# Padding the selector and the transposed weights of a windowed attention from 48 to 128 rows

## The reference, cut to what matters

```python
ak = (ax @ WK_w + WK_b).reshape(Bx, 1, nh, d)
av = (ax @ WV_w + WV_b).reshape(Bx, 1, nh, d)
pad_k = jnp.pad(k, ((0, 0), (1, 1), (0, 0), (0, 0)))
k_shift = jnp.stack([pad_k[:, t:Lx + t] for t in range(3)], axis=3)
K = jnp.concatenate([akb, k_shift], axis=3)
V = jnp.concatenate([avb, k_shift], axis=3)
scores = jnp.einsum('blhd,blhjd->blhj', q, K) / jnp.sqrt(jnp.float32(d))
alphas = jax.nn.softmax(scores, axis=-1)
att = jnp.einsum('blhj,blhjd->blhd', alphas, V).reshape(Bx, Lx, nh * d)
return att @ WO_w + WO_b
```

## Time and profile before

| | us |
|---|---|
| median of 3 runs | 2455.49 (2452.77 to 2458.71) |
| the profiled execution, device time | 2449.27 |
| its span, first to last instruction | 2447.5 |
| the attention stage that the change touches | about 740 to 1127 of the span |

### The profile page before, as it was taken

One profiled execution on the slowest core, in us unless ns is written; L12 is line 12 of the kernel. 1 busy time (PEld: TensorE's weight loads), 2 busy tenths in 40 slices (PEclk: granted clock), 3 DMA queues, 4 the chain that ended last, 5 costly groups with the idle time before them and its releaser, 6 DMA issues.

```text
span 2447.5 us, 74401 instructions
## 1 busy us (share of the span) xinstructions
PE 2164.3 (88%) x31577; PEld 1391.1 (57%) x31577; DVE 1746.2 (71%) x4002; ACT 1072.9 (44%) x2881; POOL 455.4 (19%) x791
## 2 busy tenths in 40 slices
PE   7999898899778889887899999967888789999988
PEld 5555544444454545453566666755665567777665
DVE  3443598999656777776777877826888667777776
ACT  2333255666531112112555555543444455555544
POOL 2211000000003242332011111244231111111100
PEclk9899799999787888876999999958999689999999
DMA  2000000000100000002111111016452211111111
GB/s 57 4 3 4 1 1 1 1 2 1 36 16 2 3 2 3 2 2 78 52 37 37 41 41 38 26 27 125 92 98 50 61 37 49 39 40 40 40 48 31
DMA packets 76109, 77.47 MB, mean 32 GB/s; under 512 B 15768, under 2 KB 57072, under 8 KB 74192
## 3 DMA queue, kind: packets, MB, share of 16 engines
q1 hardware_dynamic: 71872, 70.21, 11.3%
q10 hardware_dynamic: 3904, 2.49, 0.3%
HBM read 60.19 MB, written 11.82 MB: 29 GB/s over the span
## 4 chain that ended last, share of the span: by engine, by line
PE 32%; DVE 14%; ACT 6%; issue 4%; DMA 1%; SPq 0%; POOL 0%; ACTq 0%; DVEq 0%; POOLq 0%
PE B L85 31%; DVE work L2031 4%; DVE work L107 2%; ACT hr L103 2%; DVE work L2035 1%; DVE hr L2022 1%; ACT L103 1%; ACT ltc L103 1%; ACT work L103 1%; ACT catt L103 1%; DVE lpq L107 1%; DVE lth L107 1%; ACT lth L103 1%; DVE catt L2326 0%; DVE lh L107 0%
## 5 line engine op out<-in xcount | busy, mean ns | idle before, releaser
L85 PE MATMUL B<-gr,wres 128*128 128x512 f32 x1248 | 380.0, 428 | 30.9 <-DVE work L107 12.7
L85 PEld LDWEIGHTS B<-gr,wres 128*128 128x128 f32 x1248 | 230.3, 194 | 113.8 <-DVE work L107 39.3
L2076 POOL COPY G<-lh 128x32 f32<-128x32 f32 x256 | 148.0, 578 | 770.5 <-DVE lh L107 770.5
L103 ACT ACTIVATE work<-B 128x512 f32<-128x512 f32 (+5 forms) x460 | 233.7, 525 | 111.8 <-PE B L85 53.9
L85 PE MATMUL B<-work 128*128 128x128 bf16 (+3 forms) x1408 | 260.7, 313 | 16.9 <-ACT work L103 7.0
L103 ACT ACTIVATE hr<-work 128x512 fp32r<-128x512 f32 x272 | 175.0, 644 | 195.9 <-DVE work L107 111.3
L85 PEld LDWEIGHTS B<-work 128*128 128x128 bf16 (+2 forms) x1408 | 142.1, 127 | 137.7 <-issue 80.1
L2022 DVE TENSOR_TENSOR hr<-work,hr 128x512 fp32r<-128x512 f32 x272 | 186.6, 686 | 35.2 <-ACT hr L103 35.0
L2031 DVE TENSOR_TENSOR work<-work 128x512 f32<-128x512 f32 x256 | 178.4, 697 | 36.2 <-ACT work L103 30.7
L107 DVE SCALAR_TENSOR_TENSOR work<-work,cw 128x512 f32<-128x512 f32 x240 | 179.1, 746 | 5.9
L85 PE MATMUL B<-hr,wres 128*128 128x512 f32 x624 | 179.2, 396 | 0.2 <-DVE hr L2022 0.2
(11 more groups left out here) (259 smaller groups left out, 3884.5 us busy)
## 6 DMA issues: line engine op xcount, KB each, us to landing
work<-wdr SPq DMA_DIRECT2D x128, 256.0 KB, 3.1
scr<-catt SPq DMA_DIRECT2D x144, 64.0 KB, 2.1
work<-scr SPq DMA_DIRECT2D x16, 384.0 KB
work<-scr SPq DMA_DIRECT2D x16, 192.0 KB
catt<-in_L_ffn_ew SPq DMA_DIRECT2D x24, 128.0 KB, 2.3
work<-scr SPq DMA_DIRECT2D x16, 128.0 KB
out<-work SPq DMA_DIRECT2D x32, 64.0 KB, 2.2
work<-in_x ACTq DMA_DIRECT2D x2, 512.0 KB, 5.3
```

The costliest lines, as they stand in the source:

```text
L85: return e.matmul(out, lhsT, rhs, start=start, stop=stop, skip_group_check=True)
L103: return e.activation(out, in_, func, bias=bias, scale=scale)
L2076: e.tensor_copy(self.G[:, :, t], self.lh[:, t % 4, :]).then_inc(*inc("l.pool", "h", li, t))
```

## The change

`selc` and `AT` get 128 rows in place of 48. The memset of `selc` zeroes all its rows, and the three selections run over all of them (they write no further ones). `AT` is zeroed once per worker by a new memset on GpSimd at the start of the stage. ScalarE's copies write rows 0 to 47 as before, and the first three of each worker wait for that memset. The spreads thus contract over 128 rows, of which the 80 added ones are zero on both sides. The number of instructions on TensorE, their order, their outputs and their columns stay.

```diff
-        self.selc = sb("selc", [48, 16, 64], BF16)
+        self.selc = sb("selc", [128, 16, 64], BF16)
...
-                            "A": ar(128, 4 * 3, 48, dt=BF16), "AT": ar(48, 3, 512, dt=BF16),
+                            "A": ar(128, 4 * 3, 48, dt=BF16), "AT": ar(128, 3, 512, dt=BF16),
...
-                act(e, m["AT"][:, j, :], Bt[0:48, 0:512], ACT.Copy).then_inc(*inc(a, "AT", i, j))
+                if i == 0:
+                    e.wait_ge(*at(f"cd{wk}.pool", "zero"))
+                act(e, m["AT"][0:48, j, :], Bt[0:48, 0:512], ACT.Copy).then_inc(*inc(a, "AT", i, j))
...
         e.memset(KP[:, :, :, 129:130], 0.0).then_inc(*inc(f"cd{wk}.pool"))
+        e.memset(m["AT"], 0.0).then_inc(*inc(f"cd{wk}.pool", "zero"))
```

## The result

The changed kernel takes 2417.63 us (median of 4 runs, 2415.03 to 2425.09) against 2454.13 us before (median of 4): a ratio of 0.9855, 95% interval 0.9827 to 0.9883. That is 36 us faster, clearly outside the range of 2430 to 2457. The forecast had the sign and one of two causes. The other cause, a pause at each passage between a product of few rows and a full one (0.20 us on the way from a spread into `gr,hr` or `wo`, and 0.10 back, at 2.4 GHz), was not in it. Nor did the clock follow the rows alone: in the last piece of the stage it was 0.54 with 64 rows, 0.78 with 72 and 0.88 with 128. The profiled execution took 2415.03 us with a span of 2413.3.

A forecast was written before the change was run, and what follows sets the result against it. TensorE was taken as the fullest engine, its clock held low by 48-row spreads. Gains of 5.5 + 4 + 2.5 + 1 = 13.0 us took 2455.5 to 2442.5 us, range 2430 to 2457.

The forecast's parts named there:

- the last piece: End of the stage, spreads alternating with `wo`: a block falls from 3.39 to 2.7 us, eight blocks gain 5.5 us.
- The sign and the direction of the clock: In the stage, TensorE's clock rises earlier with 128-row spreads and time falls by 5 to 26 us; chance 0.81.
- The memsets: New memsets on GpSimd, 1.4 us each, under a wait for a DMA: cost 0, without this cover 2 x 1.4.
- The spreads themselves: The stage's 192 spreads keep their columns: 0 for the length, at the ends 2.5 us lost and nothing gained.
- The third rival: Slower: 128-row spreads might keep the next weights from loading beside them; at most 19 us, giving 2465; chance 0.04.
- The other half of each pair of units: 0: From worker 0's transposes to worker 1's: VectorE sets this half; more clock is worth 0, at most 1 us each.
- the stretch at 748: Near 748 us, VectorE already at 3.64 of 4 us, so little to gain: 1 us, bounds 0 and 2.
- The turns from worker 1 to worker 0: Worker 1's transposes to worker 0's next unit: 4 us at 890 to 904, 2.5 one unit earlier, 0 near 996.
- The low end: Whole kernel: 2430, the sum with all gains at their bounds (26 us, which would be 2429).

The follow-up runs named there:

- probe: Kernel before plus 960 back-to-back bf16 matmuls on TensorE ahead of the GRU, in runs of 96 at one row count; 48 rows: clock from 1.00 to 0.50.
- probemix: Kernel before plus 960 such matmuls, with two row counts in turn in some runs; 96 took 30.4 to 30.5 us (32, 48 or 64 against 128), 20.7 (72).

## Why the prediction was wrong

**The sign and the direction of the clock: right; the reason for it: right in part.** The prediction put the low clock of 1096 to 1122 down to the spreads' 48 rows, and every term of its sum rests on a clock that rises when they fill 128. The added rows do bring the clock up, zeros or not (the stage from 0.78 to 0.88 and 0.89), and the probe shows that 48 rows alone let it fall, from 1.00 to 0.50. But how the throttle arrives at its clock no row and no run shows, and rows alone do not account for it: the last piece, from which the forecast started, still stood at 0.54 with 64 rows, and came up to 0.78 with 72, when the pauses were gone. With 128 rows it went as forecast: the stretch that stood at 0.50 from 1096 to 1122 now reads

```profile
1064.00:1068.00 4.00, 3.14 (x9) 0.95 (x8) 3.90 (x7) 0.69 (x1) 2.04 (x2) 1.00 0.00 0
1068.00:1072.00 4.00, 2.88 (x9) 1.16 (x10) 3.37 (x6) 0.00 (x0) 3.92 (x4) 1.00 0.00 0
```

with a clock of 1.00 while spreads and `wo` alternate, and GpSimd as the engine that sets the step. (From 1076 to 1080, behind a wait, it is down to 0.64 once more.) GpSimd's timeline there, against the earlier trace rows:

```profile
1067.23 1.27 POOL L1518 TENSOR_TENSOR work<-work 128x512 f32<-128x512 f32 x1
1068.46 1.27 POOL L1514 TENSOR_TENSOR work<-work 128x512 f32<-128x512 f32 x1
1069.81 1.27 POOL L1518 TENSOR_TENSOR work<-work 128x512 f32<-128x512 f32 x1
1071.03 1.27 POOL L1514 TENSOR_TENSOR work<-work 128x512 f32<-128x512 f32 x1
```

Additions follow each other without idle time, and a block takes 2.57 us (1068.46 to 1071.03), where 2.7 was forecast for 3.39. One wait of 3.85 us behind TensorE is left at 1078.71. The piece gained 5.5 us of 5.5. The exact match is partly luck: 4.6 of it came with the step from 64 to 72 rows, for which the forecast had no cause, and the piece was 36.6 us and not 35.7 in the second profile of the changed kernel.

**The memsets: right.** `AT` took 1.38 us for each worker (1.4 forecast), and the kernel with the memsets alone stood at 1.0001 of before (0.9977 to 1.0025).

**The spreads themselves: the step that failed first.** It compared a matmul's own length over 48 and 128 rows, which is indeed the same (0.387 and 0.389 us medians), and took 0 for the change. The price lay between matmuls, 0.20 us at each passage from a spread to `gr,hr` or `wo` and 0.10 at each passage back. The third rival had the right place and the wrong sign: it feared that weights load beside a narrow product, and not beside a full one. They load beside either, as long as both products are narrow or both are full (in the probe, with 48 rows behind 48 and with 128 behind 128, the load begins 2 ns behind the start of the matmul ahead). At the passage from a spread of 48 rows to `wo` it began 0.32 us behind (857.58 above). The rival was turned down with the step from one spread to the next (0.22 us). That pair has no passage in it. The pair that had to be looked at, a spread and a `wo` behind it, shows 0.32 us in the trace of before, at 857.26 and 857.58 above; and a product of 128 rows followed by another stood beside it in the same trace at 0.23 (`gr,hr` to `gr,hr`). Pieces of the profile were there, and not put beside each other. The 124 passages of the stage, put at 19 us above as an estimate, and what their going did for the clock are most of the difference between 13 and 36 us.

**"The other half of each pair of units: 0": wrong, by 19 us.** The four pieces gained 20.2 us, where the stretch at 748 was put at 1 and all else at 0. The argument was that the slowest clock (0.70) went with the shortest stretch (42 us). But those stretches were cut by eye, at 944 and 986. The transposes are at 940.7 and 989.1, and the piece is 48.4 us long at 0.69, the longest of the four. Cut at the same instruction each time, slow clock and long piece go together, which says the reverse of what was read. Nor did VectorE set this half. It was busy 32.3 of 43.7 us, and its two large groups stood idle behind TensorE for 10.1 us. Those groups in 838.5 to 882.2 before (busy, mean ns, idle before):

```profile
L107 DVE SCALAR_TENSOR_TENSOR work<-B,ckc,work 128x512 f32<-128x512 f32 x20 | 14.8, 742 | 4.5 <-PE B L85 4.5
L1470 DVE TENSOR_TENSOR work<-B,work 128x512 f32<-128x512 f32 x21 | 14.2, 679 | 5.6 <-PE B L85 5.6
```

and in 830.8 to 869.7 after (where a releaser is called remote, the trace lacks the record that it belongs to):

```profile
L107 DVE SCALAR_TENSOR_TENSOR work<-B,ckc,work 128x512 f32<-128x512 f32 x20 | 14.7, 741 | 1.5 <-PE B L85 1.5
L1472 DVE TENSOR_TENSOR work<-B,work 128x512 f32<-128x512 f32 x21 | 14.2, 679 | 4.3 <-remote 4.3
```

The idle time fell from 10.1 to 5.8 us, and the piece by 4.8.

**The turns from worker 1 to worker 0: 6.5 forecast, 12.1 measured.** The three gained 4.0, 4.4 and 3.7 us. Two were put at 2.5 and 4, the third at 0, since its clock was low before its spreads began. The pauses are in all three, and they were missing from each term.

**The low end.** 2430 was the sum of all bounds. Bounds on the terms of one mechanism don't bound a second one. The price of a passage should have stood among the unknowns, with a gain as one of its ends; the step from 64 to 72 rows puts it, with what it does to the clock, at some 22 us of the stage, or 19 us by the times of whole executions.

## What to carry to other kernels

In this case a spread over 48 rows was as long as one over 128 (0.387 and 0.389 us), and cost two things more. An unbroken stream of 48-row matmuls let TensorE's clock fall from 1.00 to 0.50. And where products of 16 to 64 rows alternated with full ones, each passage cost 0.10 us, and 0.20 on the way from a spread of 48 or 64 rows into `gr,hr` and `wo`. Rows of zeros up to 72 removed the passages' price, and up to 128 gave back more of the clock (the stage's mean from 0.84 to 0.88), for a memset of 1.38 us per worker on GpSimd. When reading a trace, compare steps between starts for each pair of neighbours, and over whole sequences, not lengths of matmuls, and cut stretches that are to be compared at the same instruction.

## What the runs showed of the hardware

- 96 matmuls over 48 rows, back to back at full busy time, brought the clock from 1.00 to 0.50; with 64, 72 and 96 rows it stayed at 1.00 (probe). 48 and 128 in turn kept 1.00, 16 and 128 in turn fell to 0.50, with a mean of 0.54 (probemix). In the kernel, the last piece stood at 0.54 with spreads of 64 rows and at 0.78 with 72.
- Between a bf16 product of 16 to 64 rows and one of 128 the step at 2.4 GHz is 0.32 us instead of 0.22, in both directions (probemix); with 16 rows at 1.2 GHz 0.54 instead of 0.43. Between 72 and 128 rows it is 0.218 us (probemix). From a spread of 48 or 64 rows into `gr,hr` or `wo` the price was 0.20 us, and 0.10 back.
- Behind a spread of 72 or 128 rows the weight load of `gr,hr` or `wo` begins within 0.01 us of that spread's start, behind one of 48 rows 0.32 us after it. Where 48 rows follow 48 (probe), the load again begins within 0.01 us. Back from `gr,hr` to a spread it begins 0.33 us after the start of the matmul ahead with 48 rows, 0.23 with 72 or 128.
- For the clock, identity tiles and tiles with a one in every second value count alike (48 rows: 0.59 and 0.58; 128 rows: 1.00). So do added rows with zeros on both sides and with ones on one (stages of 356.2 and 356.3 us).
